# Two attention layers, a gated-expert layer and a routed-expert layer on one core: matrix products of the identity in TensorE's gaps

## The reference

```python
x = x + attention_A(layernorm(x), ctx)        # 1 head of 256, keys and values from the 1601 context rows
x = x + experts_B(layernorm(x))               # 8 causal heads of 64; per token and head one of 8 value and output experts
x = x + attention_C(layernorm(x), ctx, mask)  # 16 heads of 16, masked, then an output projection
x = x + experts_D(layernorm(x))               # 32 experts of 192, best 8 per token, capacity 256 rows of each expert
```

```python
probs = softmax(x @ gate_weight.T); topw, topi = top_k(probs, 8); topw /= topw.sum(-1)
buf[e, pos] = x            # each of a token's 8 choices to its expert's buffer, in the order of the tokens
h = silu(buf @ gate) * (buf @ up); eo = h @ down
out[token] = sum over its 8 choices of topw * eo[e, pos]
```

## Time and profile before

| | |
|---|---|
| Median of 3 runs | 2170.24 us (2167.64 to 2173.86) |
| The profiled execution: time | 2150.47 us |
| its span, first to last instruction | 2148.7 us |
| mean granted TensorE clock | 0.979 of full speed |
| TensorE busy with products (PE) | 2006.7 us, 93% of the span, 10241 instructions |
| TensorE weight loads (PEld) | 1098.4 us, 51% |
| VectorE, ScalarE, GpSimd busy | 1267.0, 815.5, 530.9 us |
| Stages in us from the span's start | `attentions_ab` 124 to 1112, `attention_c` 1113 to 1937, `experts` 1938 to 2148 |

### The profile page before, as it was taken

One profiled execution on the slowest core, in us unless ns is written; L12 is line 12 of the kernel. 1 busy time (PEld: TensorE's weight loads), 2 busy tenths in 40 slices (PEclk: granted clock), 3 DMA queues, 4 the chain that ended last, 5 costly groups with the idle time before them and its releaser, 6 DMA issues. The chain is left out here.

```text
span 2148.7 us, 27323 instructions
## 1 busy us (share of the span) xinstructions
PE 2006.7 (93%) x10241; PEld 1098.4 (51%) x10346; DVE 1267.0 (59%) x2532; ACT 815.5 (38%) x1636; POOL 530.9 (25%) x456
## 2 busy tenths in 40 slices
PE   6989999999999999989989999999999999995994
PEld 3656467755677467845653333333343333334773
DVE  3523864357624764368777677777777777742342
ACT  2422211221112211111116667666766676661220
POOL 5211000210001000000025224225522541235675
PEclk9999999999999999999999999999999999997997
DMA  9751000110001000020226293326434533104987
GB/s 312 204 224 62 1 1 1 51 46 1 0 20 62 0 1 1 11 61 16 40 71 116 75 284 82 79 52 164 104 79 85 138 70 49 50 26 164 289 189 164
DMA packets 101532, 184.98 MB, mean 86 GB/s; under 512 B 38152, under 2 KB 62550, under 8 KB 100121
## 3 DMA queue, kind: packets, MB, share of 16 engines
q1 hardware_dynamic: 83000, 153.24, 26.7%
q0 software_dynamic: 18400, 30.00, 6.0%
HBM read 127.38 MB, written 65.25 MB: 90 GB/s over the span
## 5 line engine op out<-in xcount | busy, mean ns | idle before, releaser
L2140 DVE CUSTOM_DVE_ANT_0 ps<-ps,maskN 128x801 f32<-128x801 f32 x480 | 468.2, 1013 | 179.0 <-PE ps L1924 179.0
L2113 ACT ACTIVATE d_prob<-ps 128x512 f32<-128x512 f32 (+1 forms) x832 | 460.3, 597 | 251.8 <-PE ps L1957 250.7
L855 PE MATMUL ps<-vx_or_keys,b_xT 128*128 128x512 f32 x512 | 241.6, 599 | 8.1 <-DVE val_or_prob L1192 8.0
L839 PE MATMUL ps<-oxB,og_or_pT 128*128 128x256 f32 x1024 | 240.2, 380 | 0.0
L1969 PE MATMUL ps<-d_prob,vaug 128*32 128x512 f32 (+1 forms) x1664 | 224.1, 604 | 0.3 <-ACT d_prob L2113 0.3
L1956 PE MATMUL ps<-maskT,identb 128*128 128x512 bf16 (+1 forms) x577 | 222.5, 386 | 1.9 <-ACT d_prob L2113 0.9
L839 PEld LDWEIGHTS ps<-oxB,og_or_pT 128*128 128x128 f32 x1024 | 190.1, 190 | 34.9 <-issue 7.7
L1956 PEld LDWEIGHTS ps<-maskT,identb 128*128 128x128 bf16 (+1 forms) x658 | 64.8, 98 | 258.5 <-ACT d_prob L2113 204.4
L268 POOL DMA_INDIRECT table<-xr,slot x128 | 128.3, 1002 | 190.6 <-PE ps L1957 159.0
L1078 ACT ACTIVATE prob_or_gate<-ps,b_mx 128x512 f32<-128x512 f32 (+3 forms) x128 | 66.0, 524 | 278.1 <-DVE b_mx L1183 278.1
L1192 DVE TENSOR_TENSOR val_or_prob<-ps,b_gm 128x512 f32<-128x512 f32 x128 | 88.3, 690 | 92.1 <-PE ps L855 92.0
(11 more groups left out here) (320 smaller groups left out, 2794.0 us busy)
## 6 DMA issues: line engine op xcount, KB each, us to landing
c_rawT<-in_maskT SPq DMA_DIRECT2D x24, 512.0 KB
vx_or_keys<-k_parts SPq DMA_DIRECT2D x60, 200.1 KB, 7.1
k_parts<-x_k SPq DMA_DIRECT2D x16, 600.4 KB
table<-xr POOLq DMA_DIRECT2D x16, 578.0 KB
e_buf<-table SPq DMA_DIRECT2D x32, 289.0 KB, 3.5
raw<-in_mask SPq DMA_DIRECT2D x10, 800.5 KB, 4.3
vx_or_keys<-in_D_w SPq DMA_DIRECT2D x12, 640.0 KB, 5.2
e_w<-in_D_w SPq DMA_DIRECT2D x12, 640.0 KB, 5.4
```

Of the source, the lines that this page charges most:

```text
L839: mm = pe.matmul(ps[:, 6 + t // 2, (t % 2) * D:(t % 2 + 1) * D], og[:, e, t * P:(t + 1) * P], oxB[:, p, e, :], start=first and t % 2 == 0, ...
L855: mm = pe.matmul(ps[:, bank, :], xTB[:, c, t * P:(t + 1) * P], vxB[:, c, h, :], start=c == 0, stop=c == NC - 1)
L2113: nc.scalar.activation(prob[0:w, T % 2, h, :], ps[0:w, BANKS[GH * T + h], :], ACT.Exp, scale=SCALE_C).then_inc(exped, 1)
L2140: v.tensor_tensor_reduce(banks, banks, maskN[:, t, MO[half]:MO[half] + w], 1.0, -3.0e38, ALU.add, ALU.max, mp[:, t, h, half:half + 1]).the ...
```

## The change

A helper issues n products of the identity with itself, into one bank of PSUM that nobody reads at that time. No wait and no semaphore goes with it. It is called at thirteen places, in the order in which they run: 14 products while the first row tile's exponentials are awaited, 10 at the end of `attentions_ab`; 9 before and 4 after `turn_maxima(0)`; 2, 3, 3 and 14 around the last steps of `attention_c`; 8, 2, 13, 46 and 3 in `experts`, before the transposes, before the logits, before `counts`, after `counts` and after the transposes of expert 0. That is 131 products.

```diff
+def idle_products(pe, k, bank, n):
+    for _ in range(n):
+        pe.matmul(k.ps[:, bank, 0:P], k.ident[:, :], k.ident[:, :], start=True, stop=True)
...
             def attention_a(b):
                 for i in range(NT + 2):
+                    if b == 0 and i == 1:
+                        idle_products(pe, k, 7, 14)
                     if 1 <= i <= NT:
...
                 attention_b(b)
+            idle_products(pe, k, 2, 10)
...
+            idle_products(pe, k, 6, 9)
             turn_maxima(0)
+            idle_products(pe, k, 6, 4)
             for G in range(NGB):
...
             values(NKT * NGB - 1)
+            idle_products(pe, k, 0, 2)
             turn_out(NGB - 1)
+            idle_products(pe, k, 0, 3)
             turn_o(NB - 1, 1)
+            idle_products(pe, k, 0, 3)
             project_last(1)
+            idle_products(pe, k, 0, 14)
...
+    IDLE = 3
...
         def _(pe):
+            idle_products(pe, k, IDLE, 8)
             for half in range(2):
...
                 mm.then_inc(r_turned, 1)
+            idle_products(pe, k, IDLE, 2)
             for t in range(NT):
...
             mm.then_inc(r.l_mm, 1)
+            idle_products(pe, k, IDLE, 13)
             r.counts(pe, LOGIT)
+            idle_products(pe, k, IDLE, 46)
...
             turn(0)
+            idle_products(pe, k, IDLE, 3)
             pe.wait_ge(k.loaded_late, 16 * (3 + KEPT))
```

## The result

The changed kernel takes 2180.64 us, median of 10 runs (2178.13 to 2188.84), beside 2171.25 us for the kernel before (2167.64 to 2176.74) in ten runs of the same job: a ratio of 1.0043 [1.0028, 1.0057]. The change makes the kernel slower by 9.4 us. The forecast was 6 us faster, and the result lies 10 us above its range.

The account below looks back on a forecast made before the run. The prediction took TensorE, busy 93% of the span, as the bound, helped only where it waits or its clock is low. Terms 2.6 + 1.4 + 0.5 + 1.5 = 6.0 us off the 2170.24 median gave 2164.2 us, range 2159.0 to 2170.5.

Parts of the forecast that it names:

- part D: 8, 2, 13, 46 and 3 products in experts: faster routing gains 1.5 us, bounds 0.5 and 2.2; the 46 counted as hidden.
- Rival 4: In experts, the 13 and 46 run at the low clock, expert 0 starts 13.1 us late: 2180.7 us, chance 0.05.
- The price of a product: One added float32 product of 128 columns, two instructions: 0.236 us at full clock, 0.47 us at the low clock.
- Rival 3: At the four places the products don't keep the clock, so time stays as before, 2170.2 us; chance 0.08.
- Part A: 14 products in batch 0's first gap, hidden; full clock speeds the next transposes and scores: 2.6 us, bounds 0 and 2.6.
- Rival 1: The clock holds in head_b(0) too, 3.4 us more gained: 2160.8 us, chance 0.18.
- Part B: 10, 9 and 4 products at attention_c's start, around turn_maxima(0): full clock gains 1.4 us, bounds 0 and 1.9.
- rival 2: Clock kept, but other engines take half of the gains at the first two places and all at attention_c's end: 2166.7, chance 0.25.
- Part C: 2, 3, 3 and 14 products at attention_c's end: faster project_last, block ends 0.5 us earlier, bounds minus 2.9 and 1.5.

Follow-up runs that it names:

- the fitted one: Changed kernel without the 10, 9 and 4 around attention_c's start and the 2 before the logits, 7 for the last 14, 9 for the 13: 2177.76 us, 1.0032.
- s: Job on a 2152 chip: kernel before 2153.33 us; with only parts A to C 2152.14, only part D 2153.09, the whole change without the 46 2149.35.
- t: Job on a 2152 chip: whole change 2149.55 us beside 2152.56 for the kernel before, ratio 0.9981; the kernel before with only the 46 2151.98.
- u: Job on a 2171 chip: kernel before (median 2171.86 us), changed kernel 2179.14, ratio 1.0038, and the fitted one 2177.76, ratio 1.0032.

## Why the prediction was wrong

**The step that failed** is part D's sentence on the 46 products: that they lie in 12.14 us of idle time, and that expert 0 "gains by the clock and hands it to nobody". As TensorE's time this held: 10.52 us, ended 1.5 us before expert 0's rows. But what they cost was not TensorE's time: the 46 alone made the kernel 15 us slower on a 2171 chip, where the sum had put them at nothing. I looked for who waits behind the products on TensorE and not for what another engine does beside the scatters. With the 46, ScalarE's pause holds up expert 0's own copy, and without them it begins only behind that copy. "Hands it to nobody" was read from a chain in which expert 7 waits for the last scatter; on a 2171 chip there is no such slack, since TensorE stands still until the scatters are over, and each expert not done before it is 4.7 us at the end. (The chain also says a little less than I read in it: 1990.87 is where the last scatter's transfer begins; it lands 4.11 us later.)

**What I could have seen.** The profile of before was 20 us under the median of its own runs. The forecast said that the rows don't show from where, and took the gain from the median as it stood. That difference was the thing that the change touched: 14 to 20 us, by which profile one compares, lie behind the last scatter, and come from the pauses beside the scatters, where the 46 were put. With a profile that doesn't stand for the timed runs, no row of it bounds a cost there, and the range should have been wider above.

**Rival 4** had the sign, with a chance of 0.05 and 2180.7 us, close to the 2180.64 measured. It isn't borne out all the same: its mechanism was a low clock under the 13 and 46. The clock was full there, the 26 instructions of the 13 took 3.15 us and the 92 took 10.52. That the number fits is chance.

**The price of a product** held: 0.236 us forecast, 92 instructions in 10.52 us and 28 in 3.29 are 0.229 and 0.235. **Rival 3** (the products don't keep the clock) fell: 1.00 at all four places. The rule of the Trainium skill ("TensorE: Matmul & The Clock Gate", Back-to-back issue gap) of 81 ns an instruction did not hold for these float32 products: they took 114 ns each over the 92.

**Part A** held: 14 products in 3.34 us, transposes 1.09, scores 5.71 (forecast 1.07 and 5.78), and `head_b(0)`'s gates at 194.94 in place of 197.56, 2.6 us. It is only as steady as the low stretch that it removes: in another execution of the kernel before that stretch is 3.4 us long and not 6.7, and the clock holds in `head_b(0)`:

```profile
135.20:138.60 3.40, 3.15 (x10) 2.44 (x11) 0.69 (x1) 0.79 (x3) 0.00 (x0) 0.50 0.98 414
138.60:145.00 6.40, 6.40 (x30) 3.85 (x29) 1.37 (x1) 0.00 (x0) 0.00 (x0) 1.00 1.01 420
197.00:204.00 7.00, 6.29 (x27) 3.93 (x28) 4.26 (x7) 1.44 (x3) 0.00 (x0) 1.00 0.00 0
```

Of the eleven profiles without part A, six are like the one of the earlier trace rows, low for 6.8 us at the gap and again in `head_b(0)`, and five like this one, 3.4 us and then full. The nine with part A have no low stretch at the gap, but eight are low in `head_b(0)` (in the profile after the clock is 0.67 over 195.0 to 204.4). The transposes of `turn_maxima(0)` begin at 1115.5 to 1118.6 us in the first case and at 1113.4 to 1114.1 in the second; with part A they begin at 1112.4 to 1114.4 in eight profiles, and at 1117.5 in the fitted one, whose clock fell at other places. So part A was worth some 2 to 3 us against the first case and next to nothing against the second; I costed it by the first alone. Rival 1 was right that whether the clock falls in the heads varies, and wrong on the side.

**Part B** went as rival 2 said. The first weighted sums come at 1119.71 in place of 1124.87 us: 3.1 of it from before the block, 2.1 from part B, where 1.4 was forecast and 1.9 was the upper bound. Some 0.4 of it comes ahead of the first score (in s, 3.5 us from the transposes to it with part B and 3.9 without), where I had counted nothing. It is given back some 130 us later: VectorE waits for a mask transfer and TensorE for VectorE. In five of the eight profiles with part B the clock falls there for 3.4 us as well, and in none of the twelve without it. By the first scatter of `attention_c` next to nothing of the 2 us is left: in t it comes at 1436.3 us in the changed kernel and at 1437.0 in the kernel before, 0.7 us apart, and they were 0.45 us apart at `turn_maxima(0)`. The rows in the profile after:

```profile
1250.21 1.00 DVE L2210 TENSOR_SCALAR maskN<-raw 128x1601 bf16<-128x1601 int32 x1 [1.51 <-DMA raw<-in_mask]
...
1252.23 0.63 PE L1934 MATMUL ps<-kS,raw 96*128 96x512 bf16 x2 [1.62 <-DVE d_mp L2156]
```

**Part C** held: `project_last` 1.97 us in place of 3.53, VectorE's last statistics at 1942.54 and TensorE's 14 products at 1943.38, so TensorE ends the block:

```profile
1938.29 1.97 PE L2027 MATMUL ps<-woC,d_oT 128*128 128x256 f32 x8
1940.09 3.29 PE L105 MATMUL ps<-ident 128*128 128x128 f32 x28
...
1942.18 0.36 DVE L2261 BATCH_NORM_AGGREGATE norm_nd_mv<-norm_nd_stats 128x2 f32<-128x6 f32 x4
```

From the last `values` to the next block's first GpSimd instruction it is 10.72 us in place of 11.24: the 0.5 us forecast. Seven products in place of 14 would end earlier than VectorE, and in the profile of the fitted version, with 7 there and 9 for the 13, it is 21.2 us from the last `values` to the first scatter in place of 22.5; its time was all the same not told apart from the changed kernel's.

**Part D without the 46** held too: logits 1.87 us in place of 3.63, `counts` delayed by the 13 (VectorE waits 0.33 us for it), and from the normalised rows to the slots 9.31 us in place of 10.85: 1.5 us, the number forecast. Parts C and D together take the stretch from the last `values` to the first scatter to 22.5 us in all five profiles that have both (the 46 apart); in the ten with neither it is 23.2 to 25.3, by where the clock fell. With D alone it is 24.0 and with A to C alone 24.1, so most of the gain of 2 us needs both; D alone gave 1.0005 [0.9993, 1.0017] as a whole.

**The sum where the kernel doesn't pause.** On the 2152 chip the whole change gave 4.1 us, with 1.5 to 6.7 as the interval; the forecast of 6.0 is inside, rival 2's 3.5 nearer to the middle. There the clock was kept where the forecast had it kept, and part B's mask and `head_b(0)` took a part back; A to C alone gave 1 us in place of 4.5. On the 2171 chips the same change pays 6.7 us and more at the pause.

## What to carry to other kernels

Work put into an engine's idle time is free only if nothing else in that stretch is already starved; ask what runs beside it, above all where GpSimd scatters and ScalarE and VectorE still have to serve TensorE. Products that keep the clock up shortened their own stretch here where they fill a gap before dense work (part A, and C with the logits), by 0.5 to 2.6 us each; how much of it reached the end of the kernel depended on where the clock fell otherwise. A long row of them before a wait that another engine ends bought nothing and carried half of the loss or more. And if the profile's execution isn't among the times of the timed runs, find out why before costing anything: here the difference was the answer.

## What the runs showed of the hardware

- The seven jobs fell into two kinds: the kernel before at 2152.5 to 2153.0 us in four jobs and at 2170.1 to 2171.9 in three, with nothing between. On the second kind ScalarE and VectorE pause beside GpSimd's 32 indirect scatters, in one to three pieces, some 24 to 34 us in all after the inputs were there (ScalarE, six profiles); the last piece ends 3.6 to 5.5 us after the last scatter is issued. GpSimd's own pace is the same on both, one scatter in 1.28 us.
- The same happens on a small scale beside the scatters of earlier batches in `attention_c`. In the changed kernel's profile (timeline):

```profile
1463.38 0.60 ACT L2129 ACTIVATE d_prob<-ps 128x512 f32<-128x512 f32 x1 [2.94 <-DMA x_ctxT<-in_ctxT]
...
1464.76 1.00 DVE L2156 CUSTOM_DVE_ANT_0 ps<-ps,maskN 128x800 f32<-128x800 f32 x1 [2.86 <-remote]
```

  There and again at 1682 it lost some 5 us each against the same program on a 2152 chip, with a low clock behind both. Its first scatter of the last batch comes at 1956.04 and that of the same kernel in u at 1950.10, which is 5.9 of the 7 us between the two spans (2181.4 and 2174.4). A run with the 46 alone lost 3 us near 1680, long before its products run, so these small pauses come without them too.
- What makes the pause isn't settled. The profile names a releaser that can't be one ("xx<-in_x", a transfer of the program's start), so the real one isn't among its events. The transfers of instructions that the trace records show nothing: around the scatters they take 0.3 to 1.5 us on either kind of chip, and none ends where a pause ends; ScalarE's own are not among them. Whether the number of TensorE's instructions or its busy time brings the pause forward is open as well, since the runs made for it met no such chip. Moving the 46 out of the stretch of the scatters altogether was not tried there.
- No version here beats the kernel before on both kinds: the best on a 2152 chip are the whole change (0.9981) and the change without the 46 (0.9989), and on a 2171 chip these are 1.0038 and 1.0019.
